# The last gated attention stage: per-key bias added by TensorE, one exponential per unit, and new interleaving orders

## Chip, cores and metric

One core of one Trainium2 chip runs the whole kernel. The metric is the device time of one launch in microseconds, as the median of several runs. PE is TensorE, with a queue of its own for weight loads (PEld); DVE is VectorE, ACT is ScalarE, POOL is GpSimd, SP is SyncE, which here only issues DMAs.

## What is computed

A decoder of four layers, each of a self-attention-like stage, a cross stage and a feed-forward stage (L0a, L0x, L0f, L1a, ... L3f), on x and a context of 8 samples x 128 tokens x 128 features. Each stage ends in `x = layernorm(x + stage(x))`. The change is in L3x, a gated retrieval with 8 heads of 16 features:

```python
log_fg = jax.nn.log_sigmoid(fgate_preact[..., 0])
cs = jnp.cumsum(log_fg, axis=-1)
fg_mat = cs[..., :, None] - cs[..., None, :]
log_D = jnp.where(mask, fg_mat + igate_preact[..., 0][..., None, :], -jnp.inf)
max_log_D = jnp.max(log_D, axis=-1, keepdims=True)
D = jnp.exp(log_D - max_log_D)
qk = jnp.einsum('bhsd,bhtd->bhst', q, k_scaled)
C = qk * D
normalizer = jnp.maximum(jnp.abs(jnp.sum(C, axis=-1, keepdims=True)), jnp.exp(-max_log_D))
C_norm = C / (normalizer + EPS)
return jnp.einsum('bhst,bhtd->bhsd', C_norm, v)
```

With a = igate - cs for a key and A for its running maximum over the keys up to a query, the exponent is a(key) - A(query), under the causal mask: a bias per key and one per query.

## The kernel before

**Work and streams.** The samples go in pairs. Two streams, a and b, each with its own tiles and its own ring of four PSUM banks, work through pairs 0 and 2 (stream a) and 1 and 3 (stream b), so that there are two turns of two pairs. A pair passes through the stages L0a to L3x (L3 feed-forward follows once, for all samples, in a block of its own at the end, L2256 on).

**What sets the order.** Each engine has one generator per stream. It yields between steps (a bank's worth of work or so), and `take_turns` (L402) walks a string written out by hand, `TURN_ORDER` (L144): "a1 b3" is one step of stream a and then three of b. There is one such string for each of PE, DVE, ACT, POOL and SP; their lengths are 724, 838, 733, 64 and 88 steps. An engine never leaves that order: where a step waits for a semaphore, everything behind it waits too. `Ring.open` (L262) makes PE wait until the bank's last use has been read by the engine named in it ("dve" or "act"). ACT's `use` and `exp_ln` (L1680, L1686) issue a table load wherever the step before left another function table, so the number of loads depends on ACT's order.

**L3x, for a pair (two samples).** Gates live in `s.gates`, with heads on partitions, sample u at rows 32u: PE multiplies context and x with the gate weights (`gate_logits_of`, L1026: the context's part at the end of L3a, x's at the start of L3x), DVE adds the biases and runs the scans (L1575 to L1586), with ACT's exponential and logarithm (L1978, L1979) between. Row 2 holds a for each key, row 5 the running maximum A, row 4 the maximum's logarithm. PE then turns rows 4 and 2 so that tokens are on partitions (two transposes, L1073, bank "mx"). ACT reads both: the exponential of row 4 (L1986) and a copy of row 2 (L1987) into `s.small[:, :, 40:48]`.

Then come four units, unit i being sample i // 2 and heads 4(i % 2) to 4(i % 2) + 3, each a PSUM bank "s" for the scores and a bank "D" for the exponent, keys on partitions, 4 heads x 128 queries in columns. PE's `units(first, second)` (L1035) fills them two at a time, (0, 3) and then (1, 2): scores (L1041), causal mask into D (L1045, bf16), and for each head -A of the query by a product of 32 rows (L1050): its stationary operand is one column of `const("pick")`, -1 at the head's row, spread over 128 columns, its moving operand is `s.gates[rows32(u), 5]`. ACT reads D four times per unit, one ACTIVATE of 128x128 for each head (L1995), because the bias of a key differs from head to head: `exp(D + bias)` with `bias=s.small[:, i // 2, h:h + 1]`. DVE multiplies scores by it (L1594) and so frees "s"; the second pair of units waits for both of those. PE multiplies the result by values (`retrieved`, L1059), ACT copies it, PE turns it back (`turned_back`, L1067), and DVE divides and normalises (L1603 to L1630), with ACT's rstd (L2003, L2004) between. `tail` ends the stage: new x_tok (L1147), transposed by PE (L441), copied by ACT (L1722).

**Neighbours that the steps touch.** `swiglu` (L684): L673 the first layers, L681 the second, ACT's L1818 the activation, DVE's L1363 and L1347. `less_maxima` (L495, L492): the same kind of product in L0x, L2x and L3a, issued over four row groups in turn; ACT's L1743 is the exponential of a whole bank there. L525 multiplies probabilities by values, L458 projects.

Of the kernel before, what the change touches and what calls it, by code (L numbers as in the profile page):

```python
# [27 lines left out]
P = 128  # L28
# [19 lines left out]
_at = 0  # L48
for _n, _w in [("ident", 128), ("neg_causal", 128), ("neg_causal_t", 128), ("causal_t", 128), ("block8", 128),
               ("ones", 128), ("spread", 128), ("tiny16", 128), ("feats", 64), ("head8in32", 4), ("head16in64", 4),  # L50
               ("pick", 8), ("cos", 8), ("sin", 8), ("eps", 5)]:
    CONST[_n] = (_at, _w)
    _at += _w
NCONST = _at
# [2 lines left out]
def shape_constants():  # L57

    c = np.zeros((P, NCONST), np.float32)
    p = np.arange(P)  # L60

    def put(name, v):
        a, w = CONST[name]
        c[:v.shape[0], a:a + w] = v.reshape(v.shape[0], w)

    put("ident", np.eye(P, dtype=np.float32))
    put("neg_causal", np.where(p[None, :] > p[:, None], NEG, 0).astype(np.float32))
    put("neg_causal_t", np.where(p[:, None] > p[None, :], NEG, 0).astype(np.float32))
    put("causal_t", (p[:, None] <= p[None, :]).astype(np.float32))
    put("block8", (p[:, None] // 8 == p[None, :] // 8).astype(np.float32))  # L70
    put("ones", np.ones((P, 128), np.float32))
    put("spread", np.tile(np.kron(np.eye(4, dtype=np.float32), np.ones((1, 8), np.float32)).reshape(1, 128), (P, 1)))
    put("tiny16", np.where(p[:, None] % 32 == p[None, :] // 8, 1e-6, 0).astype(np.float32))
    put("feats", (p[:, None] // 32 == np.arange(64) % 32 // 8).astype(np.float32))
    put("head8in32", (p[:, None] % 32 // 8 == np.arange(4)).astype(np.float32))
    put("head16in64", (p[:, None] % 64 // 16 == np.arange(4)).astype(np.float32))
    put("pick", -(p[:, None] % 32 == np.arange(8)).astype(np.float32))
    inv = np.float32(1.0) / np.float32(10000.0) ** (np.arange(0, 8, 2, dtype=np.float32) / np.float32(8))
    ang = np.concatenate([p.astype(np.float32)[:, None] * inv[None, :]] * 2, axis=1)
    sin = np.sin(ang)  # L80
    sin[:, :4] *= -1
    put("cos", np.cos(ang))
    put("sin", sin)
    put("eps", np.tile(np.array([1e-5, 1e-6, 1.0, 1e-8, -1.5 * 2 ** 23], np.float32), (P, 1)))
    return c
# [47 lines left out]
def group_words(g):  # L133
# [10 lines left out]
TURN_ORDER = {  # L144
# [12 lines left out]
    "dve":  # L157
# [10 lines left out]
    "act":  # L168
# [8 lines left out]
    "pool":  # L177
        "a1 b1 a1 b2 a3 b1 a1 b1 a1 b1 a3 b1 a1 b2 a1 b2 a1 b1 a4 b1 a2 b4 a1 b2 a2 b2 a1 b1 a3 b1 a1 b2 a1 b2 a1 "
        "b2 a2 b2 a1 b1 ",
    "sp":  # L180
        "a3 b6 a18 b12 a23 b26 ",
}
# [7 lines left out]
def _build(nc, ctx, dram, out):  # L190
# [24 lines left out]
    def const(name):  # L215
        a, w = CONST[name]
        return W["con_sts"][:, a:a + w]
# [173 lines left out]
    def rows32(g):  # L391
        return slice(32 * g, 32 * g + 32)
# [19 lines left out]
    with nc.Block(name="layers") as block:  # L412

        @block.tensor
        def _(eng):
            mm, tr = pe.matmul, pe.transpose

            def program(g):
# [611 lines left out]
                def L3x():  # L1030
# [4 lines left out]
                    def units(first, second):  # L1035
# [10 lines left out]
                        for i, b in zip(both, banks):  # L1046
                            u, half = i // 2, i % 2
                            for j in range(4):
                                h = 4 * half + j
                                m = mm(b[:, j * T:j * T + T], const("pick")[rows32(u), h:h + 1].to_broadcast([32, P]),  # L1050
                                       s.gates[rows32(u), 5], start=False, stop=j == 3)
                            filled(m, "L3x", "D", i)

                    def retrieved(u):
# [14 lines left out]

                    b = opened("act", "L3x", "mx")  # L1070
                    pe.wait_ge(*told("L3x_gates"))
                    for k, row in enumerate((4, 2)):
                        m = tr(b[:, 64 * k:64 * k + 64], s.gates[:, row], IDENT[0:64, 0:64])  # L1073
                    filled(m, "L3x", "mx")
                    yield
                    pe.wait_ge(*told("L3x_bd"))
                    units(0, 3)
# [598 lines left out]
        def _(eng):  # L1676
# [12 lines left out]
            def program(g):  # L1689
# [279 lines left out]
                def L3x():  # L1969
# [12 lines left out]
                    yield  # L1982
                    exp_ln()
                    b = bank("L3x", "mx")
                    per_head = lambda k: b[:, 64 * k:64 * k + 64].rearrange("p (u h) -> p u h", u=NS)[:, :, 0:HC]
                    o.count(act.activation(s.small[:, :, 32:40], per_head(0), ACT.Exp, scale=-1.0))  # L1986
                    link(act.copy(s.small[:, :, 40:48], per_head(1)), free("L3x", "mx"))  # L1987
                    yield
                    for i in (0, 3, 1, 2):
                        exp_ln()  # L1990
                        b = bank("L3x", "D", i)
                        for j in range(4):
                            cols = slice(j * T, j * T + T)
                            h = 40 + 4 * (i % 2) + j
                            o.count(act.activation(s.p[:, i, cols], b[:, cols], ACT.Exp, bias=s.small[:, i // 2, h:h + 1]),  # L1995
                                    free("L3x", "D", i) if j == 3 else None)
                        yield
                    for u in range(NS):
                        keep("L3x", ("oT", u), s.qk[:, u])
# [420 lines left out]
```

How the kernel before makes its waits and increments, by code:

```python
        def open(self, key, by):  # L262
            bank, self.n = self.n % len(self.banks), self.n + 1
            if self.last[bank]:
                pe.wait_ge(S(f"{self.name(bank)}_freed_{self.last[bank]}"), self.frees[bank][self.last[bank]])
            self.fills[bank] += 1
            self.frees[bank][by] += 1
            self.last[bank] = by
            assert key not in self.at, key
            self.at[key] = (bank, self.fills[bank], by, self.frees[bank][by])
            return psum[self.banks[bank]]
# [89 lines left out]
        def link(self, ins, sem=None):  # L362
            done = self.count(ins, sem)
            self.eng.wait_ge(*done)
# [1 line left out]
        def settle(self, sem=None):  # L366
            sem = sem or S(f"{self.name}_step")
            self.eng.wait_ge(sem, self.n[id(sem)])
# [68 lines left out]
                def turn_x(st):  # L437
                    b = opened("act", st, "xT")
                    pe.wait_ge(*told("x_new", NS))
                    for u in range(NS):
                        m = tr(b[:, tk(u)], s.x_tok[:, u], IDENT)
                    filled(m, st, "xT")
# [10 lines left out]
                def project(st, w, outs=None):  # L453
                    b = opened("dve", st, "y")
                    for a in outs or [(st, "o", u) for u in range(NS)]:
                        pe.wait_ge(*freed(*a))
                    for u in range(NS):
                        m = mm(b[:, tk(u)], s.attnT[:, u], w, start=True, stop=True)
                    filled(m, st, "y")
```

## Time and profile before

| | us |
|---|---|
| median of 3 runs | 1021.25 (1021.25 to 1021.33) |
| the profiled execution | 1022.06 |
| its span, first to last instruction | 1020.0 |
| PE busy | 904.2 (89%), 9368 matmul records |
| DVE busy | 539.7 (53%) |
| ACT busy | 450.7 (44%), table loads among it 97.5 |
| POOL busy | 50.8 (5%) |
| mean granted PE clock | 0.952 |

An f32 product is two matmul records in the trace, a bf16 one or a transpose one. Where the timeline merges neighbours of one line, "x16" is the number of records, and the length runs from the first one's start to the last one's end. "[2.08 <-ACT p L1818]" is idle time of the engine before the row, and what ended it. L3x runs from about 428 to 466 for pair 0, 516 to 545 for pair 1, 955 to 993 for pair 2 and 969 to 1005 for pair 3 (from the transpose L441 that ends the stage before to its own).

### The profile page before, as it was taken

Reading aid. Unit: us, or ns where it says so; the run is one execution under the profiler, and the core shown is the slowest. Engines: PE = TensorE matmul, PEld = TensorE weight load, DVE = VectorE, ACT = ScalarE, POOL = GpSimd, SP = SyncE. Lnnn points to the kernel's source line nnn. Section 1 sums busy time; section 2 is a strip of 40 time slices with the busy share of each in tenths; the row PEclk is TensorE's granted clock in tenths of the full one; section 3 lists DMA queues with packets and bytes.
Section 4 is the critical chain, followed back from the end, with each engine's and each line's share of the span. In section 5 each row is a group of like instructions: output and inputs, shape, how many; then the busy total and the mean of one; then the engine's idle time right before and its main releaser. Section 6 shows DMA issues by size and latency. Waiting matters only on the chain. (4 is left out here: it accounts for less than half of the span.)

```text
span 1020.0 us, 22561 instructions
## 1 busy us (share of the span) xinstructions
PE 904.2 (89%) x9368; PEld 700.2 (69%) x9368; DVE 539.7 (53%) x1569; ACT 450.7 (44%) x923; POOL 50.8 (5%) x71
## 2 busy tenths in 40 slices
PE   7689899999989998997987979989998989899772
PEld 5257768778778785666556757867887868686441
DVE  5733565653265575347636853655325547454345
ACT  2044343453454673574255233244465446433442
POOL 2300000010010000001000000001001000000000
PEclk8799989999999998999999999999999999999965
DMA  9100000401000301103000000040000030000000
GB/s 344 40 2 3 1 1 1 166 2 37 2 19 1 141 3 40 43 12 139 2 12 1 2 1 2 2 166 33 6 1 19 1 140 1 2 1 2 2 1 21
DMA packets 6838, 36.12 MB, mean 35 GB/s; under 512 B 721, under 2 KB 4305, under 8 KB 5458
## 3 DMA queue, kind: packets, MB, share of 16 engines
q1 hardware_dynamic: 6738, 34.68, 9.1%
q8 instruction: 76, 1.25, 0.5%
q14 instruction: 24, 0.20, 0.1%
HBM read 34.15 MB, written 0.52 MB: 34 GB/s over the span
## 5 line engine op out<-in xcount | busy, mean ns | idle before, releaser
L673 PE MATMUL bank<-xT,weights_F 128*128 128x256 f32 x832 | 202.9, 386 | 3.1 <-ACT p L1818 2.6
L673 PEld LDWEIGHTS bank<-xT,weights_F 128*128 128x128 f32 x832 | 152.0, 193 | 26.8 <-issue 4.2
L681 PEld LDWEIGHTS bank<-weights_F,p 128*128 128x128 f32 x1088 | 133.4, 191 | 18.8 <-DVE p L1363 7.2
L681 PE MATMUL bank<-weights_F,p 128*128 128x128 f32 x1088 | 141.3, 278 | 3.7 <-DVE p L1363 3.0
L1743 ACT ACTIVATE p<-bank 128x512 f32<-128x512 f32 x160 | 84.5, 601 | 121.0 <-PE bank L492 120.9
L1683 ACT ACT_TABLE_LOAD x76 | 97.5, 1283 | 12.9 <-DMA weights_con<-in_con 5.9
L1347 DVE SCALAR_TENSOR_TENSOR res<-bank,comb,res 128x128 f32<-128x128 f32 x184 | 55.7, 345 | 74.1 <-PE bank L681 71.6
L1184 DVE TENSOR_REDUCE m_wide<-bank 128x4 f32<-128x512 f32 x96 | 60.3, 684 | 43.4 <-PE bank L780 33.5
L1818 ACT ACTIVATE p<-bank 128x512 f32<-128x512 f32 x72 | 42.5, 597 | 91.6 <-PE bank L673 91.2
L1363 DVE TENSOR_TENSOR p<-p,bank 128x512 f32<-128x512 f32 x72 | 49.3, 685 | 47.5 <-PE bank L673 27.3
L1894 ACT ACTIVATE p<-bank 128x512 f32<-128x512 f32 x64 | 36.6, 598 | 51.3 <-PE bank L673 51.2
L492 PEld LDWEIGHTS bank<-mT,weights_con 32*128 32x128 f32 x1280 | 46.4, 194 | 17.4 <-issue 13.5
L492 PE MATMUL bank<-mT,weights_con 32*128 32x128 f32 x1280 | 55.1, 296 | 0.0
L1715 ACT ACTIVATE lnv<-mv,weights_con 128x2 f32<-128x2 f32 x56 | 16.6, 296 | 74.7 <-DVE mv L1139 72.7
L1192 DVE TENSOR_REDUCE mx<-bank 128x4 f32<-128x512 f32 x64 | 40.2, 682 | 16.5 <-PE bank L488 16.4
L2037 POOL TENSOR_TENSOR xb<-x_tok,biases 128x256 f32<-128x256 f32 x24 | 19.3, 806 | 575.1 <-DVE x_tok L1147 561.5
L525 PE MATMUL bank<-p,vz 128*32 128x128 f32 x1280 | 42.7, 280 | 4.5 <-ACT p L1743 4.4
L525 PEld LDWEIGHTS bank<-p,vz 128*32 128x32 f32 x1280 | 35.2, 112 | 11.0 <-issue 8.4
L525 PE MATMUL bank<-p,weights_con 128*32 128x128 f32 x1280 | 41.7, 275 | 0.0
L1207 DVE TENSOR_TENSOR attnT<-bank,res 128x128 f32<-128x128 f32 x32 | 9.3, 289 | 55.7 <-ACT res L1748 55.7
L525 PEld LDWEIGHTS bank<-p,weights_con 128*32 128x32 f32 x1280 | 35.9, 111 | 1.0
L1147 DVE TENSOR_SCALAR x_tok<-res,mv,rstd 128x128 f32<-128x128 f32 x88 | 26.4, 343 | 18.1 <-ACT rstd L1716 17.6
(319 smaller groups left out, 1356.0 us busy)
## 6 DMA issues: line engine op xcount, KB each, us to landing
weights_F<-in_L1f SPq DMA_DIRECT2D x2, 4096.0 KB, 13.8
weights_F<-in_L0f SPq DMA_DIRECT2D x2, 3456.0 KB, 13.4
weights_F<-in_L2f SPq DMA_DIRECT2D x2, 3456.0 KB, 12.1
weights_Y<-in_L1x_kv SPq DMA_DIRECT2D x2, 1024.0 KB, 10.6
weights_Z<-in_L1x SPq DMA_DIRECT2D x2, 1024.0 KB, 12.9
weights_Y<-in_L2a SPq DMA_DIRECT2D x2, 898.0 KB, 4.4
weights_Z<-in_L2x SPq DMA_DIRECT2D x2, 449.0 KB, 3.2
weights_L3m<-in_L3m SPq DMA_DIRECT2D x2, 288.0 KB, 6.1
```

The costliest lines, as they stand in the source:

```text
L492: return mm(b[:, j * T:j * T + T], const("pick")[rows32(i), j:j + 1].to_broadcast([32, P]), s.mT[rows32(i), u], start=False, stop=last)
L525: m = mm(b[rows32(g_), cols], w, probs(g_, i), start=n == 0 and i == 0 and not (part and floor is not None), stop=n == len(blocks) - 1 and ...
L673: m = mm(b[:, k * NT:(k + 1) * NT], W[weight][:, f:f + P], s.xT[:], start=True, stop=True)
L681: m = mm(b[:, tk(u)], h[:, tk(u)], w, start=k == 0, stop=k == len(chunks) - 1)
L1184: o.count(dve.tensor_reduce(s.m_wide[:, u, 32 * i:32 * i + 4], heads(b[:], 4), X, ALU.max), free(st, "s", u, 0, i))
L1192: o.count(dve.tensor_reduce(s.mx[:, u, blk, 4 * i:4 * i + 4], heads(b[:], 4), X, ALU.max), free(st, "s", u, blk, i))
L1347: dve.scalar_tensor_tensor(r, y, s.comb[:, u, e:e + 1], r if i else s.x_tok[:, u], ALU.mult, ALU.add))
L1363: o.count(dve.tensor_tensor(s.p[:, 2 + e % 3], s.p[:, e % 2], bank(st, "up", e)[:], ALU.mult), free(st, "up", e))
L1683: act.preload_act_table_set(functions)
L1743: o.count(act.activation(s.p[:, first + i], b[:], ACT.Exp, scale=scale), free(st, "t", u, blk, i))
L1818: o.count(act.activation(s.p[:, e % 2], b[:], ACT.Silu), free(st, "gate", e))
L1894: o.count(act.activation(s.p[:, 2 * (e % 3) + half], b[:], ACT.Gelu_apprx_tanh), free("L1f", f"up{half}", e))
```

## The change

PE adds the key's bias too: behind each head's product with `pick` stands a second one whose stationary operand is `s.gates[rows32(u), 2]` (a, 32 rows x 128 keys) and whose moving operand is one column of a new constant, `choose` (+1 at the head's row), spread over 128 columns. The bank then holds the whole exponent, and ACT takes it in one ACTIVATE of 128x512 per unit without a bias. The transpose of row 2 and ACT's copy of it with its wait go away. The constants grow by 8 columns, from 1125 to 1133. The steps stay as they are, and the order strings of PE, DVE, ACT and POOL are written anew from pair 1's L0x on; SP's is the same.

```diff
-               ("pick", 8), ("cos", 8), ("sin", 8), ("eps", 5)]:
+               ("pick", 8), ("choose", 8), ("cos", 8), ("sin", 8), ("eps", 5)]:
...
+    put("choose", (p[:, None] % 32 == np.arange(8)).astype(np.float32))
...
                             for j in range(4):
                                 h = 4 * half + j
-                                m = mm(b[:, j * T:j * T + T], const("pick")[rows32(u), h:h + 1].to_broadcast([32, P]),
-                                       s.gates[rows32(u), 5], start=False, stop=j == 3)
+                                mm(b[:, j * T:j * T + T], const("pick")[rows32(u), h:h + 1].to_broadcast([32, P]),
+                                   s.gates[rows32(u), 5], start=False, stop=False)
+                                m = mm(b[:, j * T:j * T + T], s.gates[rows32(u), 2], const("choose")[rows32(u), h:h + 1].to_broadcast([32, P]),
+                                       start=False, stop=j == 3)
...
-                    for k, row in enumerate((4, 2)):
-                        m = tr(b[:, 64 * k:64 * k + 64], s.gates[:, row], IDENT[0:64, 0:64])
-                    filled(m, "L3x", "mx")
+                    filled(tr(b[:, 0:64], s.gates[:, 4], IDENT[0:64, 0:64]), "L3x", "mx")
...
-                    per_head = lambda k: b[:, 64 * k:64 * k + 64].rearrange("p (u h) -> p u h", u=NS)[:, :, 0:HC]
-                    o.count(act.activation(s.small[:, :, 32:40], per_head(0), ACT.Exp, scale=-1.0))
-                    link(act.copy(s.small[:, :, 40:48], per_head(1)), free("L3x", "mx"))
+                    per_head = b[:, 0:64].rearrange("p (u h) -> p u h", u=NS)[:, :, 0:HC]
+                    o.count(act.activation(s.small[:, :, 32:40], per_head, ACT.Exp, scale=-1.0), free("L3x", "mx"))
...
                         b = bank("L3x", "D", i)
-                        for j in range(4):
-                            cols = slice(j * T, j * T + T)
-                            h = 40 + 4 * (i % 2) + j
-                            o.count(act.activation(s.p[:, i, cols], b[:, cols], ACT.Exp, bias=s.small[:, i // 2, h:h + 1]),
-                                    free("L3x", "D", i) if j == 3 else None)
+                        o.count(act.activation(s.p[:, i], b[:], ACT.Exp), free("L3x", "D", i))
```

The last steps of PE's order, with the work that each string puts there (pair 2 is a, pair 3 is b):

```
before: a L1073 | a units(0,3) | b L458 | b L1026 ctx | b L441 | a units(1,2) | b L1026 x | a L1059 x2 | a L1067 x2 | b L1073 | b units(0,3) | b units(1,2)
after:  a L1073 | b L458 | b L1026 ctx | a units(0,3) | b L441 | b L1026 x | a units(1,2) | b L1073 | b units(0,3) | a L1059 x2 | a L1067 x2 | b units(1,2)
```

Around pair 0's L3x (pair 1 is b, in L2f): before, L673 of the next expert stood ahead of a's L1073 and units(0,3), and now it stands behind them; ACT's step L2003 of a, which stood between b's last two activations (L1818), now stands ahead of both. Around pair 1's L3x PE's order is unchanged. In the L1a and L1x stages the steps of stream b stand up to 11 steps of a earlier in the first turn and up to 16 later in the second; in L0f of the first turn up to 15 later.

## Rows read from the trace of the kernel before

**Rows 1.** The page, part 1: busy us, share of the span, instructions.

```profile
PE 904.2 (89%) x9368; PEld 700.2 (69%) x9368; DVE 539.7 (53%) x1569; ACT 450.7 (44%) x923; POOL 50.8 (5%) x71
```

**Rows 2.** Groups by line and shape: busy us, mean ns, idle before and releasers.

```profile
L673 PE MATMUL bank<-xT,weights_F 128*128 128x256 f32 x832 | 202.9, 386 | 3.1 <-ACT p L1818 2.6 <-ACT p L1894 0.5
...
L1683 ACT ACT_TABLE_LOAD x76 | 97.5, 1283 | 12.9 <-DMA weights_con<-in_con 5.9 <-PE bank L525 5.5 <-PE bank L908 0.2
L1743 ACT ACTIVATE p<-bank 128x512 f32<-128x512 f32 x160 | 84.5, 601 | 121.0 <-PE bank L492 120.9
...
L492 PE MATMUL bank<-mT,weights_con 32*128 32x128 f32 x1280 | 55.1, 296 | 0.0
```

**Rows 3.** Timeline, pair 0's L3x beside pair 1's L2f: start, length (us), what, [idle before].

```profile
439.50 0.28 DVE L1586 TENSOR_TENSOR wide<-wide 64x128 f32<-64x128 f32 x1
...
439.89 1.84 PE L673 MATMUL bank<-xT,weights_F 128*128 128x256 f32 x4 [2.08 <-ACT p L1818]
...
444.30 1.71 PE L1050 MATMUL bank<-wide,weights_con 32*128 32x128 f32 x16
445.55 2.17 ACT L1995 ACTIVATE p<-bank,small 128x128 f32<-128x128 f32 x8 [3.13 <-PE bank L1050]
...
447.74 1.28 ACT L1683 ACT_TABLE_LOAD   x1
447.85 0.68 DVE L1594 SCALAR_TENSOR_TENSOR p<-bank,p 128x512 f32<-128x512 f32 x1
...
461.55 1.28 ACT L1683 ACT_TABLE_LOAD   x1
...
464.78 1.16 PE L681 MATMUL bank<-weights_F,p 128*128 128x128 f32 x8 [1.97 <-DVE p L1363]
```

**Rows 4.** Timeline, pair 1's L3x beside pair 2's L0x.

```profile
528.76 1.13 PE L1041 MATMUL bank<-wide,ctxT 64*128 64x512 f32 x4 [0.84 <-DVE p L1594]
...
535.01 1.09 ACT L1743 ACTIVATE p<-bank 128x512 f32<-128x512 f32 x2 [1.29 <-PE bank L492]
```

**Rows 5.** Timeline, pairs 2 and 3 in L3x.

```profile
962.25 1.12 PE L1041 MATMUL bank<-wide,ctxT 64*128 64x512 f32 x4
...
965.47 0.71 PE L458 MATMUL bank<-weights_L3a,attnT 128*128 128x128 f32 x4
...
969.25 0.37 ACT L1722 COPY xT<-bank 128x256 f32<-128x256 f32 x1 [1.23 <-PE bank L441]
...
974.13 0.63 PE L1026 MATMUL bank<-xT,weights_L3x 128*32 128x128 f32 x8
...
976.59 1.94 PE L1059 MATMUL bank<-p,v_ones 128*32 128x128 f32 x32 [1.83 <-DVE p L1594]
...
978.37 0.28 DVE L1586 TENSOR_TENSOR wide<-wide 64x128 f32<-64x128 f32 x1
...
979.69 0.37 PE L1073 MATMUL bank<-weights_con,wide 64*128 64x64 f32 x1
...
987.17 2.08 PE L1041 MATMUL bank<-wide,ctxT 64*128 64x512 f32 x4 [2.59 <-DVE p L1594]
...
990.14 3.09 PE L1050 MATMUL bank<-wide,weights_con 32*128 32x128 f32 x16
...
994.46 0.69 DVE L1594 SCALAR_TENSOR_TENSOR p<-bank,p 128x512 f32<-128x512 f32 x1 [0.34 <-ACT p L1995]
```

**Rows 6.** Windows: from:to, length, busy us (x instructions) by engine, clock, DMA.

```profile
187.60:269.00 81.40, 77.87 (x809) 65.33 (x805) 38.51 (x108) 38.11 (x71) 2.96 (x2) 1.00 0.12 50
670.50:747.20 76.70, 72.07 (x738) 59.53 (x735) 35.35 (x97) 38.41 (x69) 2.96 (x2) 1.00 0.13 54
123.60:187.60 64.00, 58.51 (x489) 46.48 (x488) 40.40 (x111) 23.10 (x42) 1.45 (x2) 0.95 0.06 20
591.10:670.50 79.40, 74.28 (x885) 58.76 (x881) 42.01 (x113) 27.35 (x60) 1.46 (x2) 0.98 0.05 16
...
500.00:550.00 50.00, 40.48 (x737) 28.47 (x735) 21.79 (x73) 23.88 (x70) 1.32 (x4) 0.99 0.03 7
```

More of the change, by code:

```diff
@@ L146 @@
         "a1 b1 a2 b1 a2 b1 a2 b3 a1 b1 a1 b1 a1 b2 a1 b2 a3 b1 a2 b1 a1 b2 a1 b1 a1 b2 a1 b1 a1 b1 a2 b1 a6 b1 "
[10 rows of a table removed]
-    "dve":
[10 rows of a table removed]
-    "act":
[8 rows of a table removed]
[10 rows of a table added]
+    "dve":
[9 rows of a table added]
+    "act":
[8 rows of a table added]
     "pool":
-        "a1 b1 a1 b2 a3 b1 a1 b1 a1 b1 a3 b1 a1 b2 a1 b2 a1 b1 a4 b1 a2 b4 a1 b2 a2 b2 a1 b1 a3 b1 a1 b2 a1 b2 a1 "
-        "b2 a2 b2 a1 b1 ",
+        "a1 b1 a1 b2 a3 b1 a1 b2 a3 b1 a2 b2 a1 b2 a1 b1 a4 b1 a2 b4 a1 b2 a2 b2 a1 b1 a2 b1 a2 b2 a1 b2 a1 b2 a2 "
+        "b2 a1 b1 ",
     "sp":
```

55 rows, old and new, of the table TURN_ORDER are left out of this document.

## The prediction

> **What bounds the kernel now.** I read the page's busy times first. PE is busy 89% of the span and both other large engines about half of it [rows 1]: work added to PE is paid for unless it falls into a gap of PE, and work taken from ACT gains only where PE waits for ACT. Next the groups by line, for the durations of what is added and removed [rows 2]. Then the timeline around the four places where the last gated stage (L3x) runs: pair 0 beside pair 1's L2f [rows 3], pair 1 beside pair 2's L0x [rows 4], pairs 2 and 3 together at the end [rows 5]. In the first two the reader is to see PE with only short gaps; in the third a chain through all engines, with PE waiting for DVE's multiply (L1594) and running at the lower of its two clock levels. Last, the windows of the stretches whose orders change most [rows 6].
>
> **The change, part by part.**
>
> *Products added on PE.* Each of 16 units gets four products of 32x128 by 128 columns, each recorded as two matmuls. The 16 records of a pair of units take 1.71 us now, 0.107 each [rows 3]. The new ones have the same shape, row group and bank, so they queue behind the old: 1.71 us more per pair of units, 8 pairs of units, 13.7 us of PE in all at 2.4 GHz. At 1.2 GHz the same 16 records took 3.09 us [rows 5]. No row shows a moving operand that is one column spread over 128; the nearest row is L1050 itself, so I take its 0.107 us. Lower bound: overlap with another row group, as L492's four groups do (1280 records busy 55.1 us, 0.043 each [rows 2]), which would make it 0.7 us per pair of units; upper bound: the half-clock price, 3.1.
>
> The Trainium skill (TensorE: Matmul & The Clock Gate, Part 3, The mechanism) says that small products overlap where their row groups differ. By it alone the added ones would cost nearly nothing; but pick and choose of a unit read the same 32 rows, and the trace has L1050 at over twice L492's time per record.
>
> *Exponentials merged on ACT.* Per pair of units eight ACTIVATEs of 128x128 ran 2.17 us [rows 3]; two of 128x512 take 0.60 each [rows 2]. ACT is released of 1.0 us per pair of units, 8 us in all. What counts is when DVE's second multiply can end. Now: L1050 starts, the first exponential 1.25 us later, the second multiply ends 4.2 after the start (444.30 to 448.53 [rows 3]). After: the second bank is full after 32 records, 3.4 us, plus about 0.4 to the exponential's start (1.25 less eight records), 0.60, and 0.69 for the multiply: 5.2. So the chain through a pair of units becomes 1.0 us longer, although ACT works less: the exponential now waits for the bank.
>
> *Removed.* One transpose per pair (one of two records of L1073, four in all) and one small ACT copy with the wait behind it. Only PE's counts; at 0.1 us a record, and two of the four where PE's order sets the time, -0.2 us. The constants grow from 1125 columns to 1133, 0.7% of one early transfer: nothing.
>
> *Pair 0.* Two pairs of units add 3.4 us of PE where PE is nearly full. The new PE order sets the first pair of units ahead of an L2f expert's first layer (L673), whose first four records now run ahead of the wait for ACT. The units can't start before the gates of L1586 are there (439.78), as late as the wait ended before (439.89), so these four records, 1.0 us at L673's 0.24 a record [rows 2], move behind it [rows 3]. Against that, ACT's new order puts L2f's last two activations next to each other, so that the load of 1.28 us at 461.55 needn't stand right before one; PE's wait of 1.97 for it [rows 3] should shrink by 1.5. Sum 3.4 + 1.0 - 1.5 = +2.9, bounds +1.4 and +4.4.
>
> *Pair 1.* PE's order is the same here. The first pair of units adds 1.71, of which the wait of 0.84 before the next [rows 4] takes up a part, but the chain through L1594 asks 1.0: +1.0. The second adds 1.71 in front of the other stream's L492, for which ACT waits 1.29 and PE's next values wait in turn [rows 4]: +1.7. Sum +2.7, bounds +2.1 and +3.4.
>
> *Pairs 2 and 3.* Cost and new order meet. Now pair 3's gate product L1026 starts at 974.13, although its xT was copied by 969.62: PE was in pair 2's second pair of units [rows 5]. The new order issues pair 3's L458 and context product ahead of pair 2's first units, and L1026 ahead of its second. By the rows: first units from 963.9 (1.3 us of moved work ahead, 0.71 and 0.63) to 968.9 (3.3 us before, plus 1.7); xT copied behind the second exponential at 970.3; L1026 at 970.4, 3.7 us earlier; second units 971.0 to 976.1; pair 3's L1073 at 976.2 where it was 979.68, its gates being ready before that (L1586 ends 3.9 us after L1026 does, at 974.9). Its first units end at 981.3. Then stand pair 2's L1059 and L1067, 3.1 us as now (976.59 to 979.69), and pair 3's second units start at 984.4, not 987.17: 2.8 earlier. From there to the end of the second multiply the trace has 8.0 us (987.17 to 995.15). After: 1.6 + 3.4 + 0.4 + 1.3 = 6.7 at 2.4 GHz; 3.0 + 6.2 + 0.6 + 1.3 = 11.1 at 1.2 GHz. So the end comes 4.0 us earlier or 0.4 later. All behind it is a chain of DVE and ACT with the same lengths; what is moved ahead of it (pair 2's normalisation, L1627 to L1637) fits in the time that PE and ACT take to turn the result back. Bounds -4.0 and +0.4; I take -1.5, since PE's two waits before that point get shorter but one stays.
>
> The skill's same page (What's actually happening) says that the clock follows how busy PE has been. In this trace the records of L1050 that follow the wait of 2.59 us take 3.09 us, at half clock, where those of pair 0 take 1.71 [rows 3, 5]. By the rule a busier PE would hold 2.4 GHz and the end would gain the whole 4.0; what it then comes to is a rival below.
>
> *Orders elsewhere.* From pair 1's L0x on, steps of the two streams change places by up to 16 turns. In the L1a and L1x stages the new first turn has nearly the interleaving of the old second turn, and the reverse. The trace has both: the four stretches leave PE 3.5, 4.6, 5.5 and 5.1 us idle [rows 6], so neither is clearly better. Walking ACT's order with each step's table gives 71 loads where there were 76 [rows 2]: 6.4 us less of ACT, mostly beside PE work. I take -1.0. Bounds: -6.4 (every load on PE's path) and +4 (as if a fifth of the 18.7 us of idle time came again). DMA and SP's order stay; POOL's differs by three steps of one place, and POOL is busy 5%.
>
> **Sum.** 2.9 + 2.7 - 1.5 - 0.2 - 1.0 = +2.9 us. The profiled execution took 1022.06 us beside a median of 1021.25, so 1024.96 in its terms and about 1024.2 for the median. A change under 0.2% (2.0 us) can't be told from none.
>
> **The rivals.**
>
> *Faster: the new orders win.* Place: the expert stages L0f, L1f and L2f, where ACT switches between its two tables. Price: 1.28 us per load on PE's path. If all five removed loads were on it, and the same idle time returned nowhere, -6.4 instead of -1.0: 1018.8. It decides from three loads on, together with the full gain at the end. For it: L673's waits for ACT's L1818 and L1894 [rows 2]; against: the four stretches have little idle time left. The Trainium skill (ScalarE: Activation LUTs, What ACT_TABLE_LOAD costs) counts about 2.66 us per switch with a drain; by it five would be 13.3 us. Here the load of 447.74 stands 20 ns behind the ACTIVATEs that end at 447.72 [rows 3]: no drain shows, and 1.28 is the whole price. Chance 0.28.
>
> *No change: the clock holds.* With 2.4 GHz through the end, the term is -4.0 instead of -1.5: 1021.7. For it: fewer waits of PE from 962 on. Against: at 984 PE waits for two copies of ACT once more. Chance 0.23.
>
> *Much slower: nothing is absorbed.* All 13.7 us on the path and no gain at the end, or a spread column that is read slowly: 1021.25 + 13.7 = 1035. Against: PE is idle 9.5 us between 500 and 550 alone [rows 6]. Chance 0.07.
>
> *The change doesn't do what it says.* The merged exponential needs the whole bank, so it may start later than the last of the four ended before. That is so at 1.2 GHz only; it is in the forecast.
>
> **The numbers.** Forecast, slower: 0.42, its own range 1023.3 to 1027. With the much slower case, slower 0.49; no change 0.23; faster 0.28. The range reaches down to 1018, which holds most of the faster case, and up to 1030, the bounds of pair 0, pair 1 and the end together (+1.5, +0.7, +1.9) with some of the orders': about 0.2 is left out.
>
> **What would show it.** 256 records of pick and choose together, and 3.4 us per pair of units; the first exponential of a pair about 0.85 us later after L1050's start than now; ACTIVATEs of 0.60 in place of L1995; 71 loads. Pair 3's L1026 on xT before pair 2's second units. DVE's multiply waiting longer in pair 1. PE's busy time up by 10 to 14 us. The forecast is wrong if PE's idle time shrinks by as much as its work grows, if the L3x of pair 1 is no longer than before, or if the clock of the last 20 us is 1.0.

## The result, and the profile after

The changed kernel took 1029.39 us (median of 7 runs, 1029.05 to 1034.58) beside 1021.25 us (median of 7, 1019.62 to 1026.75) for the one before: ratio 1.008, 95% interval 1.0053 to 1.0108, so about 8 us slower. Forecast were 1024.2, with 1018 to 1030 as the range. The direction and the range held. The size did not come about as the sum has it: three of its terms were wrong, two by +4.4 and +3.0 us and one by -4.0, and the experiments show two large effects of opposite sign behind the whole.

The page, busy us by engine, against [rows 1]:

```profile
span 1027.4 us, 22751 instructions
PE 921.2 (90%) x9492; PEld 720.0 (70%) x9492; DVE 540.5 (53%) x1569; ACT 436.2 (42%) x866; POOL 51.0 (5%) x71
```

PE is busy 17.0 us longer, where 13.7 at full clock were added. ACT works 14.5 us less, and the kernel is slower all the same.

Groups by line (busy us, mean ns, idle before), against [rows 2]:

```profile
L1683 ACT ACT_TABLE_LOAD x71 | 91.1, 1283 | 8.2 <-DMA weights_con<-in_con 5.6
...
L1050 PE MATMUL bank<-wide,weights_con 32*128 32x128 f32 x128 | 25.0, 303 | 0.0
L1052 PE MATMUL bank<-weights_con,wide 32*128 32x128 f32 x128 | 24.3, 291 | 0.0
```

The 71 loads and the 128 new records (L1052) are as worked out; a product with the spread column as moving operand costs the same as one with it as stationary operand.

**Where the time went.** The transposes L441 that end each stage of stream b give the account (start in us, before and after):

| stage ended | before | after | difference | step |
|---|---|---|---|---|
| L2x, pair 1 | 423.1 | 423.9 | +0.8 | |
| L2f, pair 1 (covers pair 0's L3x) | 469.3 | 473.0 | +3.7 | +2.9 |
| L3a, pair 1 | 516.1 | 517.8 | +1.8 | -1.9 |
| L3x, pair 1 | 544.8 | 553.7 | +8.9 | +7.1 |
| L3a, pair 3 | 968.8 | 974.6 | +5.8 | -3.1 |
| L3x, pair 3 | 1005.3 | 1012.6 | +7.3 | +1.5 |

Pair 1's stage and what is behind it. The timeline of the changed kernel there, against [rows 4] (start, length, what, idle before and its releaser):

```profile
517.92 0.60 ACT L1743 ACTIVATE p<-bank 128x512 f32<-128x512 f32 x1 [2.95 <-PE bank L492]
...
518.81 1.70 ACT L1974 ACTIVATE wide<-xT,weights_con 128x256 f32<-128x256 f32 x4
...
520.90 0.30 ACT L1978 ACTIVATE wide<-wide 64x128 f32<-64x128 f32 x1
521.23 0.40 ACT L1979 ACTIVATE wide<-wide,weights_con 64x128 f32<-64x128 f32 x1
521.53 1.05 ACT L1743 ACTIVATE p<-bank 128x512 f32<-128x512 f32 x2
...
522.84 3.64 PE L525 MATMUL bank<-p,vz 128*32 128x128 f32 x64 [3.37 <-ACT p L1743]
...
529.06 0.27 PE L1074 MATMUL bank<-weights_con,wide 64*128 64x64 f32 x1
...
530.71 0.48 PE L1050 MATMUL bank<-wide,weights_con 32*128 32x128 f32 x2
...
532.79 0.60 ACT L1991 ACTIVATE p<-bank 128x512 f32<-128x512 f32 x1 [2.74 <-PE bank L1052]
```

Before the change the same product of probabilities and values waited 0.56 us:

```profile
518.74 1.95 PE L525 MATMUL bank<-p,vz 128*32 128x128 f32 x64 [0.56 <-ACT p L1743]
```

From L441 (517.83) to the transpose of the gates, L1074, the changed kernel takes 11.2 us, the one before 6.7; from there to the end of the stage 24.7 against 22.1. The second part is the forecast's term (+2.6 measured, +2.7 forecast). The first is not in the prediction: ACT's new order puts pair 1's L1974, L1978 and L1979 between the other stream's exponentials (L1743), so PE's L525 waits 3.37 us for the last of them, and then runs at half clock (3.64 us for 64 records, where they took 1.95).

The end, against [rows 5]:

```profile
975.67 1.07 PE L1026 MATMUL bank<-xT,weights_L3x 128*32 128x128 f32 x8 [0.58 <-ACT xT L1722]
...
983.06 0.36 PE L1074 MATMUL bank<-weights_con,wide 64*128 64x64 f32 x1
...
986.14 0.79 PE L1050 MATMUL bank<-wide,weights_con 32*128 32x128 f32 x2
```

The steps came in the order forecast: L1026 at 975.67, ahead of pair 2's second units (their products start at 979.23), and L1074 behind them. But the windows of the same stretch (from:to, length, busy us (x instructions) of PE, PEld, DVE, ACT, POOL, clock, DMA) show what the clock did:

```profile
442.70:446.30 3.60, 3.60 (x34) 3.39 (x33) 0.69 (x1) 0.60 (x1) 0.00 (x0) 1.00 0.00 0
976.70:982.20 5.50, 5.50 (x37) 3.57 (x36) 3.01 (x11) 1.96 (x5) 0.00 (x0) 0.81 0.00 0
982.20:995.80 13.60, 13.60 (x82) 9.66 (x81) 2.51 (x4) 2.61 (x6) 0.00 (x0) 0.50 0.01 1
```

PE has no gap in these records from 976.7 to 995.8, and yet it runs at 1.2 GHz from 982.2 to 995.8. The 32 records of a pair of units take 3.49 us in pair 0 (442.79 to 446.28) and 6.51 at 986.14. From 974.6 to 1012.6, pair 3's last stage, the time is 38.0 us where it was 36.5.

The clock fell in pair 0 too, right behind the first pair of units (mean granted clock 0.50 from 446.3 to 449.7, again without a gap of PE). The expert's L673 stands there, and its eight records take 3.68 us; in the kernel before eight of them took 1.89 (from 446.93).

```profile
446.22 3.68 PE L673 MATMUL bank<-xT,weights_F 128*128 128x256 f32 x8
```

### The profile page after: what moved, and what is told of

The parts are those of the page before. It is cut to its first block and busy times, and to the rows that moved or that the text cites. A ratio compares the mean times of both kernels' runs of the same rounds, so it can differ in the third digit from the quotient of the medians.

```text
span 1027.4 us, 22751 instructions
## 1 busy us (share of the span) xinstructions
PE 921.2 (90%) x9492; PEld 720.0 (70%) x9492; DVE 540.5 (53%) x1569; ACT 436.2 (42%) x866; POOL 51.0 (5%) x71
## 5 line engine op out<-in xcount | busy, mean ns | idle before, releaser
L673 PE MATMUL bank<-xT,weights_F 128*128 128x256 f32 x832 | 204.5, 389 | 1.7 <-ACT p L1818 1.7
L673 PEld LDWEIGHTS bank<-xT,weights_F 128*128 128x128 f32 x832 | 153.8, 195 | 23.9 <-issue 3.0
L1743 ACT ACTIVATE p<-bank 128x512 f32<-128x512 f32 x160 | 84.0, 602 | 124.9 <-PE bank L492 124.8
L1818 ACT ACTIVATE p<-bank 128x512 f32<-128x512 f32 x72 | 42.6, 597 | 95.3 <-PE bank L673 94.9
L492 PEld LDWEIGHTS bank<-mT,weights_con 32*128 32x128 f32 x1280 | 46.0, 192 | 17.7 <-issue 13.8
L492 PE MATMUL bank<-mT,weights_con 32*128 32x128 f32 x1280 | 54.6, 294 | 0.0
L525 PE MATMUL bank<-p,vz 128*32 128x128 f32 x1280 | 44.4, 287 | 8.9 <-ACT p L1743 6.9
L525 PEld LDWEIGHTS bank<-p,vz 128*32 128x32 f32 x1280 | 36.6, 115 | 17.6 <-issue 14.8
L525 PE MATMUL bank<-p,weights_con 128*32 128x128 f32 x1280 | 43.1, 281 | 0.0
L525 PEld LDWEIGHTS bank<-p,weights_con 128*32 128x32 f32 x1280 | 36.9, 113 | 1.2 <-issue 0.2
## 6 DMA issues: line engine op xcount, KB each, us to landing
weights_F<-in_L2f SPq DMA_DIRECT2D x2, 3456.0 KB, 11.3
```

What stands on the lines that cost most here:

```text
L492: return mm(b[:, j * T:j * T + T], const("pick")[rows32(i), j:j + 1].to_broadcast([32, P]), s.mT[rows32(i), u], start=False, stop=last)
L525: m = mm(b[rows32(g_), cols], w, probs(g_, i), start=n == 0 and i == 0 and not (part and floor is not None), stop=n == len(blocks) - 1 and ...
L673: m = mm(b[:, k * NT:(k + 1) * NT], W[weight][:, f:f + P], s.xT[:], start=True, stop=True)
L1743: o.count(act.activation(s.p[:, first + i], b[:], ACT.Exp, scale=scale), free(st, "t", u, blk, i))
L1818: o.count(act.activation(s.p[:, e % 2], b[:], ACT.Silu), free(st, "gate", e))
```

## The experiments

All were timed in 5 rounds beside the kernel before on the same chip. The medians of the kernel before in the three groups were 1022.32 (runs 1 to 4), 1022.26 (5 to 8) and 1023.51 us (9 to 12), so the ratios, not the medians, are compared across groups. The first 90 us, which no change touches, differ by up to 8 us between profiled executions, so profiles are compared by stretches only.

**First question: the edit or the orders?** Run 1 is the changed kernel with all the order strings of the kernel before, run 2 the kernel before with all the new ones. One line of PE's string stands for them (run 1; run 2 the reverse):

```diff
-        "b15 a1 b3 a2 b1 a1 b2 a2 b2 a2 b1 a1 b1 a1 b1 a1 b2 a1 b2 a1 b2 a6 b7 a1 b1 ",
+        "b2 a1 b6 a1 b15 a1 b3 a2 b1 a1 b2 a2 b2 a2 b1 a1 b1 a1 b1 a2 b3 a1 b1 a6 b3 a1 b7 ",
```

> The edit with the order strings of the kernel before. Theory (the edit costs PE time, and the new orders add their own cost in two places): pair 0 and pair 1 cost about 2.9 and 2.6 us as computed, and at the end the chain costs 1.0 us at 2.4 GHz and 3 at 1.2 GHz for each pair of units of pair 3, so 6 to 9 us over the kernel before: ratio 1.006 to 1.009. L525 of pair 2 beside pair 1's L3x runs at 2.4 GHz as before, 1.95 us for 64 records. Rival (the new orders do most of the harm): ratio 1.002 or less.

Measured: 1038.63 us (1036.43 to 1040.0), ratio 1.0166 (1.0139 to 1.0193), twice what the theory allows, and further still from the rival.

> The code of the kernel before with the new order strings. Theory: ACT's new order beside pair 1's L3x holds back two exponentials of pair 2, PE waits over 3 us and the clock falls, 4 to 5 us; the end gains 2 to 3 from the earlier gate product; the rest is within 3 either way: ratio 1.000 to 1.004. Rival (the orders fit each other elsewhere and are a gain by themselves): 0.997 or less.

Measured: 1015.35 us (1008.4 to 1016.79), ratio 0.9918 (0.9888 to 0.9948). The rival holds, not the theory.

The small change is the sum of two large ones. The edit alone costs 17 us, more than the 13.7 of added records; the orders alone gain 8. Under the new orders it costs 17 too by the ratios (1.008 less 0.9918), 14 by the medians of the two groups. By the ends of stages, run 1 loses 5.7 us in pair 0, 4.3 in pair 1 and 8.0 at the end; two of its last three pairs of units take 6.50 and 6.51 us, at half clock. In run 2 a pair of units takes 1.71 us as before, and 3.09 twice. Its pair 0 is 1.6 us shorter than before and its pair 1 is 4.7 longer.

**Which part of the edit?** Run 3 is run 1 with the merged exponential taken apart, run 4 is run 1 without the products that were added, so the key's bias is missing from its result.

```diff
-                        o.count(act.activation(s.p[:, i], b[:], ACT.Exp), free("L3x", "D", i))
+                        for j in range(4):
+                            cols = slice(j * T, j * T + T)
+                            o.count(act.activation(s.p[:, i, cols], b[:, cols], ACT.Exp, bias=const("eps")[:, 5:6]),
+                                    free("L3x", "D", i) if j == 3 else None)
```

> The edit with the old orders, but ACT still takes four exponentials of 128x128 per unit, with a bias of zero from a constant. Theory: the longer PE time is the whole cost and merging gains little, since the exponential waits for the full bank either way: the second multiply of a pair of units ends 1.25 + 1.7 + 1.1 + 0.7 us after L1050's start, 0.5 us later than with the merged ones; so 1 to 4 us slower than the edit with the old orders. Rival (ACT's release matters for the other stream, 1.0 us for each of 8 pairs of units): 6 us or more slower than the edit with the old orders.

Measured: 1042.66 us (1037.04 to 1044.26), ratio 1.0194 (1.0163 to 1.0224).

```diff
-                                mm(b[:, j * T:j * T + T], const("pick")[rows32(u), h:h + 1].to_broadcast([32, P]),
-                                   s.gates[rows32(u), 5], start=False, stop=False)
-                                m = mm(b[:, j * T:j * T + T], s.gates[rows32(u), 2], const("choose")[rows32(u), h:h + 1].to_broadcast([32, P]),
-                                       start=False, stop=j == 3)
+                                m = mm(b[:, j * T:j * T + T], const("pick")[rows32(u), h:h + 1].to_broadcast([32, P]),
+                                       s.gates[rows32(u), 5], start=False, stop=j == 3)
```

> The old orders, one exponential of 128x512 per unit, but the products that add the key's bias are left out, so this part of the computation is missing; the transpose and the copy are gone too. Theory: 1.0 us less in the chain of each pair of units; with two pairs each for pair 1 and pair 3 on the path, 3 to 5 us faster than before, ratio 0.995 to 0.997. Rival (ACT is hidden everywhere): 0.999 to 1.001.

Measured: 1018.95 us (1013.04 to 1023.25), ratio 0.9971 (0.9948 to 0.9994).

The merged exponential is worth about 3 us by either (1.0194 less 1.0166, whose intervals overlap; 1 less 0.9971, whose interval excludes 1), of the 8 that it takes from ACT. The products cost 1.0166 less 0.9971, 20 us, one and a half times their time at full clock. The merge pays, the products in this sequence do not.

**Why are the products so dear?** Two suspects: they stand in one row group each, one behind the other; and the clock. Run 5 is the changed kernel with the products of the two banks issued in turn. The two units of a pair are of different samples, so their rows (32u and up) are different row groups; work, constants and order of steps stay.

```diff
-                        for i, b in zip(both, banks):
-                            u, half = i // 2, i % 2
-                            for j in range(4):
-                                h = 4 * half + j
+                        for j in range(4):
+                            for i, b in zip(both, banks):
+                                u, h = i // 2, 4 * (i % 2) + j
...
+                            for i, b in zip(both, banks):
+                                u, h = i // 2, 4 * (i % 2) + j
                                 m = mm(b[:, j * T:j * T + T], s.gates[rows32(u), 2], const("choose")[rows32(u), h:h + 1].to_broadcast([32, P]),
                                        start=False, stop=j == 3)
```

> The changed kernel with the products of a pair of units issued in turn over its two banks, whose operands lie in different row groups (rows 0 to 31 and 32 to 63), instead of bank by bank. Theory (the edit's cost is that its products queue in one row group): the 32 records of a pair of units take 1.7 to 1.9 us where they take 3.49 at 2.4 GHz and 6.51 at 1.2 GHz; the edit then costs next to nothing and the kernel comes to the time of the new orders alone, 1013 to 1018 us, ratio 0.990 to 0.997. Rival (products of two row groups don't run beside each other where they go to different banks in turn, or the pair's first exponential, which now waits for both banks, costs what PE gains): above 1.004.

Measured: 1009.91 us (1008.09 to 1011.88), ratio 0.9883 (0.986 to 0.9907): 20 us less than the changed kernel by the ratios (19.5 by the medians), by nothing but the sequence of 128 products, and below the range of the theory. A window at the end, and under it a line of the timeline:

```profile
978.30:980.50 2.20, 2.11 (x33) 1.86 (x32) 1.84 (x6) 0.06 (x1) 0.00 (x0) 1.00 0.00 0
```

```profile
978.36 0.49 PE L1049 MATMUL bank<-wide,weights_con 32*128 32x128 f32 x4
```

A pair of units takes 2.05 us instead of 3.49, 0.064 a record, in all eight places, and none falls to half clock. Eight times 1.44 is 11.5; 3.4 more is what the changed kernel lost beyond full-clock time in its slow units (6.51 and 3.90 instead of 3.49 each). In the profiles pair 0 is 4.3 us shorter than in the changed kernel, pair 1 3.7, and the stretch from pair 2's transpose of the gates (L1074 there) to the last L441 11.3. That what remains is other work at the lower clock fits these stretches (L673 in pair 0 among it), but was not separated. The mean granted clock from 940 us to the last instruction is 0.81 here and 0.76 there, some 26 and 42 us at half clock.

Runs 6 and 7 give the old orders and the unchanged kernel the same alternation.

> The edit with the old orders (1038 us before) and the products in turn over the two banks. Theory: back to 1018 to 1024 us, ratio 0.996 to 1.003. Rival: above 1.010.

Measured: 1024.12 us (1017.68 to 1028.64), ratio 1.0013 (0.999 to 1.0037), 16 us less than run 1 by the ratios.

> The kernel before with its own 16 records per pair of units issued in turn over the two banks. Theory: 0.9 us instead of 1.71 for the 16 records, 0.8 less for each of the 8 pairs of units, of which the chain through ACT keeps part (its first exponential waits for both banks): 1 to 5 us faster, ratio 0.995 to 0.999. Rival (PE's time in L3x is hidden): 1.000.

Measured: 1020.1 us (1014.03 to 1027.4), ratio 0.9984 (0.9959 to 1.0009). A pair of units takes 1.16 us instead of 1.71, 4.4 us in all, and at most as much comes off the total (1.6 us by the ratio, interval -0.9 to 4.2). With twice the records per pair of units the same alternation gained 16 to 20. Under the old orders, then, the edit with alternated products stands 3 us above the kernel before with alternated products (1.0013 against 0.9984, intervals overlapping).

**Is the clock a cause of its own?** Run 8 keeps the products in their order of the changed kernel, and their number, and lets each read 64 rows instead of 32. Its constants are zero in the rows of the other sample.

```diff
-                                mm(b[:, j * T:j * T + T], const("pick")[rows32(u), h:h + 1].to_broadcast([32, P]),
-                                   s.gates[rows32(u), 5], start=False, stop=False)
+                                mm(b[:, j * T:j * T + T], const("pick_u")[0:64, 8 * u + h:8 * u + h + 1].to_broadcast([64, P]),
+                                   s.gates[0:64, 5], start=False, stop=False)
...
```

> The changed kernel with its L3x products over 64 rows instead of 32 (constants that are zero in the other sample's rows), so that the same number of records of the same length fills twice the rows. Theory (a product of few rows keeps PE busy but doesn't hold its clock): the granted clock stays at 1.00 in at least one of the pairs of units at the end that now run at 0.50, where PE is never idle, and the time falls by 2 to 5 us against the changed kernel. Rival (the clock doesn't depend on rows): the same time within 1 us, with the same two or three falls of the clock after 970 us.

Measured: 1021.73 us (1019.48 to 1025.9), ratio 1.0003 (0.9983 to 1.0023): 8 us less than the changed kernel, more than the theory's 2 to 5, though each pair of units is longer (3.83 us at full clock, where 3.49 were). Windows of one stretch in the changed kernel, and under it in run 8:

```profile
966.00:992.00 26.00, 24.40 (x180) 17.26 (x173) 10.43 (x30) 7.13 (x19) 0.31 (x1) 0.75 0.01 1
```

```profile
966.00:992.00 26.00, 25.13 (x223) 18.52 (x217) 12.55 (x38) 8.71 (x21) 0.31 (x1) 1.00 0.01 2
```

PE is busy 94% and 97% of these 26 us. With 32 rows its granted clock is 0.75, with 64 rows 1.00, and PE gets through 223 records where it got through 180 (run 8 is 3 us ahead at the start of the stretch). From pair 3's L3a to the end of its L3x the changed kernel takes 38.0 us and run 8 31.1. So the busy share that the records show did not decide the clock here; the rows that the products use, the only thing changed, did. It isn't an accident of one profile: the mean granted clock of the whole kernel is 0.960 to 0.965 in all 12 runs with 64 rows and 0.943 to 0.950 in all 7 of the changed kernel. Nor is it the end alone. Right behind the first pair of units of pair 0, where the changed kernel falls to half clock, run 8 stays at 1.00, and so does run 5; the same eight records of L673 take 1.99 us in run 8 where they took 3.68:

```profile
445.12 1.99 PE L676 MATMUL bank<-xT,weights_F 128*128 128x256 f32 x8
```

**Pair 1 and ACT's order.** Run 10 is the changed kernel with the eleven ACT steps around pair 1 (pair 2's exponentials L1743 and pair 1's L1974, L1978, L1979) in the sequence of before; run 11 is run 5 with the same. The piece of ACT's string:

```diff
-"a1 b2 a1 b3 a2 b1 a1 b2"
+"a2 b1 a2 b4 a1 b3"
```

> The changed kernel, with the eleven ACT steps around pair 1 (368 to 378 of ACT's order) put back as the kernel before has them: pair 2's exponentials of L1743 ahead of pair 1's L1974 and gate exponentials again. Theory (pair 1's 4.4 us beyond the forecast come from this order: PE's L525 had to wait 3.37 us for L1743 and ran at half clock): from L441 to L1073 of pair 1 about 7 us again instead of 11.2, L525 starting with under 1 us idle, and 3 to 5 us off the total, 1.022 to 1.032 of the changed kernel's run turned into about 1.003 to 1.005 of the kernel before. Rival (what is lost there is regained later anyway, as turn 2 regained 2.9 us in the changed kernel): pair 1's stage ends 4 us sooner, the end within 1 us of the changed kernel, 1.007 to 1.009.

Measured: 1024.1 us (1019.23 to 1030.43, 12 runs), ratio 1.0014 (0.9991 to 1.0036), against 1.008 for the changed kernel, so 6.7 us less. Its timeline (the lines are one higher):

```profile
514.76 0.44 PE L442 MATMUL bank<-weights_con,x_tok 128*128 128x128 f32 x2
...
517.44 1.96 PE L526 MATMUL bank<-p,vz 128*32 128x128 f32 x64 [0.56 <-ACT p L1744]
...
521.46 0.24 PE L1075 MATMUL bank<-weights_con,wide 64*128 64x64 f32 x1 [0.31 <-DVE wide L1587]
```

The wait is 0.56 us again and the stretch from the stage's end to the gates' transpose 6.7, as before the change. That stretch is 6.7 in every one of the eight experiments that has ACT's old sequence there (runs 1, 3, 4, 6, 7, 10, 11, 12), and 10.0 to 11.4 in the four that have the new one (2, 5, 8, 9). The rival, that the loss would be regained later, is out: it came off the total. The gain of 6.7 is larger than pair 1's 4.5, though the two intervals leave room for 4.5. In the profile the rest lies at the end, where no pair of units took over 4.12 us, against 6.51; the clock's falls there changed places, and why was not tested.

> The changed kernel with both edits of its order: the 32-row products issued in turn over the two banks, and the eleven ACT steps of pair 1 as in the kernel before. If the two gains add: 3 to 5 us below the run with the alternation alone, 0.984 to 0.985 of the kernel before (1005 to 1007 us). If pair 1's loss is regained later: 0.988 as with the alternation alone.

Measured: 1005.85 us (1003.41 to 1007.67), ratio 0.9823 (0.9797 to 0.9849). The two gains add (20 and 6.7), and this version beats both kernels: by 18 us the one before, by 26 (the ratios' difference) the changed one.

**Is the edit worth keeping?** Runs 9 and 12 are runs 5 and 11 without the edit: kernel before, new orders, alternated products, in 12 with ACT's order of pair 1.

> The kernel before (its pick products alone and four biased exponentials of 128x128) with the new orders of the steps and its products issued in turn over the two banks. It tells what the edit is worth once its products are cheap. Theory (the edit was dear for its 32-row products in one row group alone; alternated, its merged exponential and the missing copy gain about 3 us): this run is 2 to 6 us slower than the edit with the same orders and the alternation, that is 0.990 to 0.994 of the kernel before. Rival (the edit gains nothing, the alternation makes both cheap): within 1 us of it or faster, 0.985 to 0.989.

Measured: 1013.0 us (1011.26 to 1013.78), ratio 0.9894 (0.9871 to 0.9917).

> The run before (no edit, new orders, products in turn over the banks) with pair 1's eleven ACT steps as in the kernel before. With the new orders alone pair 1 had lost 4.6 us: if that is ACT's order, pair 1 is 4 us shorter here than in the run without it, and the total 2 to 4 us less, 0.986 to 0.991; if it is regained later, the same total.

Measured: 1009.63 us (1007.54 to 1015.78), ratio 0.9869 (0.984 to 0.9899).

On the same chip, run 11 with the edit stands 3.8 us below run 12 without it (0.9823 against 0.9869; the intervals overlap by 0.0009). Between runs 5 and 9 the ratios differ by 0.0011, which shows nothing. So with alternated products the edit gains between nothing and 5 us; the theory's 2 to 6 is not confirmed for the first pair and agrees with the second. Run 9 itself beats run 2 by 0.9918 less 0.9894, inside the intervals. ACT's eleven steps gained 6 us by the ratios (run 11 over run 5; 4 by the medians of the two groups) and 3 (run 12 over run 9, intervals overlapping).

## Why the prediction was right, and where it was wrong

- **Pair 0, +2.9:** measured +2.9, and part of that is luck. The records took 3.49 us a pair of units where 3.4 were forecast (two times 1.71 by [rows 3]), and no gap took them up. But the edit alone costs 5.7 here (run 1) and the orders alone gain 1.6 (run 2), where the sum has 3.4 and -0.5. L673 at half clock behind the first units, 1.8 us, is no part of the sum.
- **Pair 1, +2.7:** measured +7.1. The step that failed is "PE's order is the same here". It is, but ACT's is not: L1974's 1.70 us, L1978 and L1979 now stand among the exponentials that PE's L525 waits for. The price of the edit itself was right (2.6 of 2.7); 4.5 us came from an order that I had read for PE alone. Run 10 shows it. Under the old orders (run 1) the edit cost this pair 4.3.
- **Pairs 2 and 3, -1.5:** measured +1.5, outside the bounds of -4.0 and +0.4. The moves happened as worked out. What failed is that the second case, half clock for 11.1 us, was priced for the last pair of units alone, from [rows 5]; it came to pair 3's first units, 6.51 us in place of 3.49, and to all around them from 982.2 to 995.8. What the moves are worth shows in the runs without the edit: this stage gains 0.3 us in run 2 and, with alternated products, 5.2 in runs 9 and 12, against the kernel before; of the 5.2, the alternation alone gives 3.0 (run 7).
- **The rule on the clock.** The Trainium skill (TensorE: Matmul & The Clock Gate, What's actually happening) was read as "a busier PE holds 2.4 GHz". The measurement decides against that reading: 13.6 us without a gap in PE's records at 1.2 GHz, and run 8 at full clock with the same number of products over more rows. The "no change" rival rested on it.
- **Row groups.** The Trainium skill (TensorE: Matmul & The Clock Gate, Part 3, The mechanism) says that products overlap where their row groups differ. The prediction cited it with the remark that pick and choose read the same rows. That is so, but the other unit's of the same pair do not, and run 5 shows what that leaves unused: 2.05 us in place of 3.49. The lower bound from L492's records was the one within reach, by an order that the change didn't have.
- **Orders elsewhere, -1.0:** measured about -5.0, the third term that was wrong. Stream b gains 1.9 us between pair 0's L3x and pair 1's, and 3.1 between the end of pair 1 and pair 3's L3a (how much of stream a's work is done at such a point differs, so a stage's end is not the total). With -5.0 in its place, and the 0.8 by which the two profiles differ at the table's first row, the terms come to the +7.3 at the last. Run 2 puts the orders as a whole at -8, pair 1's loss of 4.7 included, so without it they would be worth some 13 (worked out, not run). The rival "faster: the new orders win" (-6.4) was right in its mechanism's sign and still too small; which of the moves carry it wasn't tried one by one.
- **The edit:** the sum gave it, without the orders, 3.4 in pair 0 and 2.7 in pair 1 and a cost at the end that the moves were to outweigh. It costs 17 us under the old orders and 14 to 17 under the new. "Much slower: nothing is absorbed" (13.7 on the path) came nearest to the mechanism and was still too small, for the clock came on top; its time didn't show because the orders gained half of it back. That the total fell into the forecast's range is luck: errors of both signs met.
- **Forecast signs that held:** the first exponential 2.08 us after L1050's start (1.25 before, 0.85 later forecast), ACTIVATEs of 0.60, PE's busy time up (by 17.0, where 10 to 14 were forecast). PE's idle time did shrink (115.8 to 106.2), which I had named as a sign against the forecast only if it shrank by all of the added work.

## What to carry over

When a change brings an edit and a new order together, run each alone: here +17 and -8 made +8. Read the new order for every engine at each place where PE waits, not for PE alone; eleven steps on ACT were worth 3 to 7 us. And small products that read a few rows belong in turn with products of other row groups: the 128 added records cost 20 us in sequence (run 1 less run 4), and with all 256 alternated the kernel stands 4 above run 4 (run 6, 1.0013 less 0.9971).

## What the runs showed of the hardware that I had not expected

Uninterrupted work didn't hold TensorE's clock. With 32-row products behind one another ahead of it (30 records in the 3.0 us before 982.2) the clock was granted at 0.50 for 13.6 us while PE was busy throughout, about half of the time with 32-row products and half with others; with 64 rows and the same number of products it was 1.00 for 26 us. Wider products, each of them slightly longer (0.120 against 0.109 us), made the kernel 8 us faster. Alternated between two row groups, records of 32x128 went from 0.109 to 0.064 us, and in the kernel before from 0.107 to 0.072. And the same instructions at the start of the kernel took up to 8 us more or less from one execution to the next (L0x of pair 0 ended 4.0 us earlier to 3.6 later than in the profile of before), which is of the size of the spread of 1017 to 1027 us that the kernel before shows; what makes it was not tested.
